# A pre-LayerNorm attention layer: the side products on TensorE cut into 64x32 pieces that stand between the two scores of a unit

## The chip, the cores and the metric

The kernel runs on one core of a Trainium2 chip. The metric is device time in microseconds (us) of the whole program, the median of the runs shown. A profile is of one execution, and its times are of that execution alone.

## What is computed

One layer over x of shape (4, 2048, 256): LayerNorm, attention with 16 heads of 16 channels, the projection added to x, a second LayerNorm, three 256x256 products in a row, tanh, added again.

```python
qkv = einsum('bse,fe->bsf', layernorm(x), in_proj_weight) + in_proj_bias
scores = einsum('bhqd,bhkd->bhqk', q / sqrt(16), k)
blocked = (j <= i) & (j >= i - 16)          # keys just before the query are left out
attn = softmax(where(blocked, -inf, scores))
x = x + einsum('bse,fe->bsf', attn @ v, out_proj_weight) + out_proj_bias
h = layernorm(x) @ ffn_weight @ ffn_aux_weight1 @ ffn_aux_weight2
return x + tanh(h + ffn_bias)
```

## The kernel before

`first_batch` prepares batch 0: LayerNorm, query, key and value projections. Then `stream` runs 16 **steps**, one for each chunk of 512 queries (4 batches x 4 chunks). A step has 64 **units** (`STEP`), numbered r = 0 to 63 here; a unit is 64 keys against 512 queries for 8 heads, 32 units for each half of the heads. On PE a unit is: first scores (`score(u, 0)`, 8 products of a 49x32 weight tile with 512 fp16 columns into two banks), the weighting of an earlier unit (`weigh`, 8 products of 64x32 with 512 fp32 columns, three or four units behind), and second scores (`score(u, 1)`, two other banks). ScalarE takes each pair of banks with one exponential of 128x1024, two a unit, 2048 in all. `score` waits for the exponential that last read its banks. VectorE multiplies out the blocked band (`mask`) in the units 15 to 23 of each half, two units behind the exponential and before the weighting. Position 13 of each half has two weightings, position 3 none.

Beside that, TensorE has **side work**, hung behind the second scores of units that `run_step` lists by number. In the first 12 steps (`PROJECTED`) it projects the chunk of the next batch: `turn` (transposes of the normalised chunk), `project_qk` for four blocks j, `project_v`, and `sum_squares` for the norms that set the softmax guard. In all steps but the first it finishes the chunk before: `project_out`, `f_turn`, `project_f`. These are 128x128 or 128x64 products over a contraction of 256, in two halves k. All of them use two spare PSUM banks, `spare[0]` and `spare[1]`, one product in each, which VectorE takes with one operation (`take_qk`, `take_v`, `take_norms`, `add_attention`, `add_f_bias`); the next user of a bank waits for that.

The order on each engine is written by hand, and a wait blocks all that stands behind it on its engine. SyncE issues all DMAs in one queue: queries for the next half, the context rows out of `raw` (`move_context`), the softmax sums and their inverses (`invert_sums`), the chunk of x for the finish (`start_chunk`), the projected parts (`store_part`), the result (`store_result`), and at a batch's end the keys of the next batch (`load_keys`, 1.5 MB for each half of the heads in pieces of few bytes: half 0 late in the last step, half 1 at the next step's start).

The lines of `run_step` on PE that set the place of side work:

```python
                    score(u, 0)
                    due = weighed_at(u)
                    if due:
                        weigh(due[0])
                    score(u, 1)
                    for w in due[1:]:
                        weigh(w)
                    if projects and r in (8, 9):
                        turn(step, r - 8)
                    if projects and r in (12, 14):
                        project_qk(step, 0, (r - 12) // 2)
```

Lines of the profile: L1135 scores, L1154 weighting, L1113 exponential, L1105 tanh, L1183 and L1248 turns, L1195 queries and keys, L1211 values, L1224 norms, L1237 output projection, L1257 last product, L837 mask, L897, L902 and L906 queries and keys on VectorE.

## Time and profile before

| | us |
|---|---|
| median of 3 runs | 2204.01 (2202.97 to 2208.4) |
| the profiled execution | 2206.76 |
| its span, first to last instruction | 2202.9 |
| ScalarE busy | 1987.1 (90%) |
| PE busy | 1903.6 (86%) |
| VectorE busy | 587.1 (27%) |

Busy time of PE counts pipelined matmuls with their whole latency, so 86% is not 86% of its peak. A float32 product shows as two matmul records and two weight loads. The loop over units runs from 87.8 to 2144.2 us; ahead of it is `first_batch`, behind it the finish of the last chunk.

### The profile page before, as it was taken

To read this page: it belongs to the slowest core of one execution; us is meant where nothing else is said; L and a number is where in the kernel's file an instruction comes from. 1 tells how busy PE (TensorE), PEld (TensorE's weight loads), DVE (VectorE), ACT (ScalarE), POOL (GpSimd) and SP (SyncE) were. 2 spreads that over 40 slices of the span, in tenths; PEclk is the share of its full clock that TensorE was granted. 3 is DMA by queue.
4 is the path that set the end of the run, shared out by engine and by line. 5 is a ranking of instruction groups with operands and counts; after the bars stand their busy time and mean duration, and the time that the engine had idled before them with its cause. 6 is when DMAs were issued, how large, how long until landed. Compare 5 with 4: busy or idle time off the path is not lost. (4 is left out here: it accounts for less than half of the span.)

```text
span 2202.9 us, 76197 instructions
## 1 busy us (share of the span) xinstructions
PE 1903.6 (86%) x34896; PEld 677.2 (31%) x34896; DVE 587.1 (27%) x1206; ACT 1987.1 (90%) x2106; POOL 149.9 (7%) x172
## 2 busy tenths in 40 slices
PE   6698998989889898999889899898988888888882
PEld 4232332323323233333323333232332222222221
DVE  5221323223222332323223232222311111111212
ACT  3499999999889999999889999999989999999990
POOL 2000101001000000101001010100100000000000
PEclk9799999999999999999999999999999999999995
DMA  3410102011240111102331010201123010101000
GB/s 120 128 31 15 44 24 63 25 54 31 44 81 24 54 33 34 44 12 63 53 67 48 24 43 24 64 24 44 32 41 64 15 44 14 44 15 34 16 23 27
DMA packets 84927, 92.81 MB, mean 42 GB/s; under 512 B 15786, under 2 KB 73578, under 8 KB 84594
## 3 DMA queue, kind: packets, MB, share of 16 engines
q1 hardware_dynamic: 84596, 87.83, 16.0%
q8 instruction: 277, 4.54, 0.9%
q14 instruction: 54, 0.44, 0.1%
HBM read 53.09 MB, written 26.25 MB: 36 GB/s over the span
## 5 line engine op out<-in xcount | busy, mean ns | idle before, releaser
L1113 ACT ACTIVATE probs<-scores 128x1024 f32<-128x1024 f32 x2048 | 1948.6, 1056 | 117.8 <-PE scores L1135 80.7
L1154 PE MATMUL outs<-probs,vs 64*32 64x512 f32 x16384 | 1081.0, 593 | 7.7 <-issue 7.7
L1135 PE MATMUL scores<-qs,ks 49*32 49x512 f16 x16384 | 839.9, 384 | 231.2 <-ACT probs L1113 180.7
L1135 PEld LDWEIGHTS scores<-qs,ks 49*32 49x32 f16 x16384 | 233.4, 89 | 1250.6 <-ACT probs L1113 1093.5
L1154 PEld LDWEIGHTS outs<-probs,vs 64*32 64x32 f32 x16384 | 291.2, 106 | 74.3 <-issue 30.7
L837 DVE TENSOR_TENSOR probs<-probs,allowed 128x320 f32<-128x320 f32 (+2 forms) x280 | 138.6, 495 | 388.1 <-ACT probs L1113 388.1
L1195 PE MATMUL spare<-s_xt,w_qkv 128*128 128x512 f32 x192 | 108.0, 645 | 0.0
L786 POOL TENSOR_TENSOR s_squares<-s_qk_f 128x512 bf16<-128x512 f32 x48 | 61.4, 1279 | 464.1 <-DVE s_qk_f L897 464.1
L1237 PE MATMUL spare<-w_o,ctx_in 128*128 128x256 f32 x256 | 74.1, 416 | 19.0 <-DVE ctx_in L862 19.0
L897 DVE TENSOR_SCALAR s_qk_f<-spare,bias_qk 128x512 f32<-128x512 f32 x48 | 36.0, 751 | 182.1 <-PE spare L1195 182.1
L1257 PE MATMUL spare<-w_ffn,s_f_xt 128*128 128x256 f32 x256 | 74.0, 415 | 0.8 <-DVE s_f_xt L977 0.8
L780 POOL TENSOR_TENSOR s_x<-s_x,bias_o 128x1024 f32<-128x1024 f32 x16 | 38.1, 2379 | 486.3 <-DMA s_x<-in_x 486.3
L845 DVE COPY raw<-outs 128x512 f32<-128x512 f32 x32 | 22.1, 692 | 172.5 <-PE outs L1154 171.6
L977 DVE COPY s_f_xt<-spare 128x512 f32<-128x512 f32 x32 | 22.1, 692 | 138.4 <-PE spare L1248 138.4
L1237 PEld LDWEIGHTS spare<-w_o,ctx_in 128*128 128x128 f32 x256 | 45.4, 196 | 38.5 <-DVE ctx_in L862 19.9
L1105 ACT ACTIVATE s_pre<-s_pre 128x1024 f32<-128x1024 f32 x16 | 17.7, 1107 | 41.2 <-DVE s_pre L983 41.2
L1211 PE MATMUL spare<-w_qkv,s_xt 128*64 128x128 f32 x768 | 53.4, 282 | 0.0
L988 DVE TENSOR_TENSOR s_pre<-s_pre,s_x 128x1024 f32<-128x1024 f32 x16 | 19.6, 1226 | 124.8 <-ACT s_pre L1105 124.8
L1257 PEld LDWEIGHTS spare<-w_ffn,s_f_xt 128*128 128x128 f32 x256 | 45.3, 196 | 19.7 <-issue 14.3
L906 DVE SCALAR_TENSOR_TENSOR s_parts<-s_qk_f,s_parts 128x512 f16<-128x512 f32 x48 | 50.2, 1045 | 0.8
L947 DVE TENSOR_TENSOR s_x<-s_x,spare 128x512 f32<-128x512 f32 x32 | 22.0, 688 | 99.7 <-PE spare L1237 99.7
L1211 PEld LDWEIGHTS spare<-w_qkv,s_xt 128*64 128x64 f32 x768 | 41.7, 138 | 15.7 <-issue 15.7
(97 smaller groups left out, 566.5 us busy)
## 6 DMA issues: line engine op xcount, KB each, us to landing
qs<-q_parts SPq DMA_DIRECT2D x192, 64.0 KB
ks<-k_parts SPq DMA_DIRECT2D x36, 256.0 KB
ctx_in<-raw SPq DMA_DIRECT2D x256, 32.0 KB, 2.0
s_x<-in_x SPq DMA_DIRECT2D x16, 512.0 KB, 4.0
inverse<-row_inverse SPq DMA_DIRECT2D x32, 256.0 KB
out<-s_pre SPq DMA_DIRECT2D x16, 512.0 KB, 2.9
s_xin<-in_x SPq DMA_DIRECT2D x12, 512.0 KB, 6.0
q_parts<-s_parts SPq DMA_DIRECT2D x24, 256.0 KB, 2.1
```

What stands on the lines that cost most here:

```text
L780: pool.tensor_tensor(x2[:], x2[:], bias, ALU.add).then_inc(biased, 1)
L786: pool.tensor_tensor(squares[:, j], qk_f[:, j % 2], qk_f[:, j % 2], ALU.mult).then_inc(squared, 1)
L837: dve.tensor_tensor(tiles, tiles, keep_row, ALU.mult).then_inc(masked, 1)
L897: dve.tensor_scalar(qk_f[:, j % 2], spare[j % 2][:], HD ** -0.5 if j < HALVES else 1.0, bias_qk[:, j:j + 1], ALU.mult, ALU.add).then_inc(q ...
L906: dve.scalar_tensor_tensor(out=parts[:, j, 1], in0=qk_f[:, j % 2], scalar=SCALE_UP, in1=parts[:, j, 0], op0=ALU.mult, op1=ALU.subtract).th ...
L1113: act.activation(probs[:, u % RING, 2 * slot:2 * slot + 2].rearrange("p c q -> p (c q)"), scores[:, 2 * slot:2 * slot + 2].rearrange("p c ...
L1135: last = pe.matmul(scores[cols, 2 * slot + e], ks[rows, group, keys], qs[rows, group], start=True, stop=True)
L1154: last = pe.matmul(outs[32 * c:32 * c + 32, side], vs[keys, at:at + 2 * HD], probs[keys, u % RING, c], start=(i == 0), stop=(i == KBLOCKS ...
L1195: last = pe.matmul(spare[j % 2][:], w_qkv[:, k, j * P:(j + 1) * P], xt[:, k], start=(k == 0), stop=(k == HALVES - 1))
L1211: last = pe.matmul(spare[1 - two // 2][side * HALF_P:(side + 1) * HALF_P, kb % 4 * P:(kb % 4 + 1) * P], xt[:, k, kb * KEYS:(kb + 1) * KEYS ...
L1237: last = pe.matmul(spare[t // 2][:, t % 2 * EMB:(t % 2 + 1) * EMB], ctx_in[:, k, t * P:(t + 1) * P], keep["w_o"][:, k], start=(k == 0), st ...
L1257: last = pe.matmul(spare[1 - t // 2][:, t % 2 * EMB:(t % 2 + 1) * EMB], f_xt[:, k, t * P:(t + 1) * P], keep["w_ffn"][:, k], start=(k == 0) ...
```

## The change

Every side product is made of pieces of the shape of the weighting: `product` and `turned_tiles` cut a 128x128 product into four column groups (32 outputs) and two row groups (64 of the contraction), 8 products that write `spare[0]` (rows 0 to 63 of the contraction) and `spare[1]` (rows 64 to 127). The two banks together now hold one product as two partial sums, and VectorE takes it with two operations, where the transposes are copied bank by bank. A piece of queries, keys, output projection or last product has 256 columns and one half k; there are four for each pair of banks. A turn's piece has 16 products of 64 columns, a piece of values 16 of 128, `sum_squares` 8 bf16 products of 512. Tables say at which unit each piece stands (25 units before, 60 now in a step that projects and finishes), and the last product of a chunk reaches into the step after the next one's start (places over 63).

In a unit with a piece PE's order is first scores, piece, second scores, weighting; in one without it stays as it was. VectorE, ScalarE (the tanh stands at unit 8 of the next step, or at 58) and SyncE follow the tables. On SyncE `store_result(step - 2)` and `start_chunk` stand behind `invert_sums`, and `move_context(step, 0)` ahead of the key parts. The folding of the three weights (`fold_ffn`, twice in step 0) keeps its 128x128 form.

```diff
+TURN_AT = (7, 8, 9, 10)
+QK_AT = ((12, 14, 15, 16), (18, 19, 20, 21), (33, 34, 35, 36), (38, 39, 40, 41))
+FOLD_AT = (23, 28)
+Y_AT = ((23, 24, 25, 26), (28, 29, 30, 31))
+V_AT = ((43, 44, 46, 47), (51, 52, 53, 54))
+NORM_AT = 49
+F_TURN_AT = {True: (56, 57, 58, 59), False: (41, 42, 43, 44)}
+F_AT = {True: ((61, 62, 63, 64), (66, 67, 68, 69)), False: ((47, 48, 49, 50), (52, 53, 54, 55))}
+SQUASH_AT = {True: 72, False: 58}
...
@@ SyncE, run_step @@
-                    start_chunk(step - 1)
                     move_context(step - 1, 1)
                     invert_sums(step - 1)
+                    if step > 1:
+                        store_result(step - 2)
+                    start_chunk(step - 1)
...
@@ VectorE, take_qk @@
-                dve.tensor_scalar(qk_f[:, j % 2], spare[j % 2][:], HD ** -0.5 if j < HALVES else 1.0,
-                                  bias_qk[:, j:j + 1], ALU.mult, ALU.add).then_inc(qk_copied, 1)
+                dve.tensor_scalar(qk_f[:, j % 2], spare[0][:], scale, bias_qk[:, j:j + 1], ALU.mult, ALU.add
+                                  ).then_inc(qk_added, 1)
+                dve.wait_ge(qk_added, n + 1)
+                dve.scalar_tensor_tensor(out=qk_f[:, j % 2], in0=spare[1][:], scalar=scale, in1=qk_f[:, j % 2],
+                                         op0=ALU.mult, op1=ALU.add).then_inc(qk_copied, 1)
...
@@ VectorE, take_norms @@
+                dve.tensor_copy(both, spare[0][0:HALF_P]).then_inc(norms_added, 1)
+                dve.wait_ge(norms_added, 2 * step + 1)
+                dve.tensor_tensor(both, both, spare[1][0:HALF_P], ALU.add).then_inc(norms_added, 1)
...
@@ PE @@
+            def turned_tiles(tiles, pair, k):
+                for t in (2 * pair, 2 * pair + 1):
+                    for c in range(4):
+                        for part in range(2):
+                            rows = slice(part * HALF_P, part * HALF_P + HALF_P)
+                            at = (k * TPC + t) * HALF_P
+                            last = pe.matmul(spare[part][32 * c:32 * c + 32, at:at + HALF_P],
+                                             tiles[rows, t, k * P + 32 * c:k * P + 32 * c + 32], ident[rows, rows],
+                                             start=True, stop=True)
+                return last
+
+            def product(at, weights, moving, k):
+                for c in range(4):
+                    for part in range(2):
+                        rows = slice(part * HALF_P, part * HALF_P + HALF_P)
+                        last = pe.matmul(spare[part][32 * c:32 * c + 32, at:at + EMB], weights(rows, c), moving[rows],
+                                         start=(k == 0), stop=(k == HALVES - 1))
+                return last
...
@@ PE, project_qk @@
+                n, k = divmod(i, HALVES)
...
+                    else:
+                        pe.wait_ge(qk_copied, step * 4 + j)
+                last = product(n * EMB, lambda rows, c: w_qkv[rows, k, j * P + 32 * c:j * P + 32 * c + 32],
+                               xt[:, k, n * EMB:(n + 1) * EMB], k)
...
@@ PE, run_step @@
-                    score(u, 0)
                     due = weighed_at(u)
-                    if due:
-                        weigh(due[0])
-                    score(u, 1)
-                    for w in due[1:]:
-                        weigh(w)
...
+                    score(u, 0)
+                    if has_piece(step, r):
+                        piece(step, r)
+                        score(u, 1)
+                        for w in due:
+                            weigh(w)
+                    else:
+                        if due:
+                            weigh(due[0])
+                        score(u, 1)
+                        for w in due[1:]:
+                            weigh(w)
```

The order on PE in step 1, from the second scores of unit 12 to the first half of block 0's second piece in unit 14, before. The names are written<-read; a count stands for equal neighbours:

```order
L1135 MATMUL scores<-qs,ks 32x512 x8
L1195 MATMUL spare<-s_xt,w_qkv 128x512
L1135 MATMUL scores<-qs,ks 32x512 x8
L1154 MATMUL outs<-probs,vs 32x512 x8
L1135 MATMUL scores<-qs,ks 32x512 x8
L1154 MATMUL outs<-probs,vs 32x512 x8
L1135 MATMUL scores<-qs,ks 32x512 x8
L1154 MATMUL outs<-probs,vs 32x512 x8
L1135 MATMUL scores<-qs,ks 32x512 x8
L1195 MATMUL spare<-s_xt,w_qkv 128x512
```

The same place now, from unit 11's second scores on:

```order
L1172 MATMUL scores<-qs,ks 32x512 x16
L1230 MATMUL spare<-s_xt,w_qkv 32x256 x8
L1172 MATMUL scores<-qs,ks 32x512 x8
L1191 MATMUL outs<-probs,vs 32x512 x8
L1172 MATMUL scores<-qs,ks 32x512 x8
L1191 MATMUL outs<-probs,vs 32x512 x8
L1172 MATMUL scores<-qs,ks 32x512 x8
L1191 MATMUL outs<-probs,vs 32x512 x8
L1172 MATMUL scores<-qs,ks 32x512 x8
L1230 MATMUL spare<-s_xt,w_qkv 32x256 x8
L1172 MATMUL scores<-qs,ks 32x512 x8
```

The piece moved from behind a unit's second scores to between its scores, and the weighting of such a unit moved behind the second scores.

VectorE in a later step, from the turned chunk to the first block of queries, before:

```order
L889 COPY s_xt<-spare 128x512 x2
L862 TENSOR_TENSOR ctx_in<-ctx_in,inverse 128x512 x2
L897 TENSOR_SCALAR s_qk_f<-spare,bias_qk 128x512
L902 TENSOR_SCALAR s_parts<-s_qk_f 128x512
L906 SCALAR_TENSOR_TENSOR s_parts<-s_qk_f,s_parts 128x512
L837 TENSOR_TENSOR probs<-probs,allowed 128x4x16
L837 TENSOR_TENSOR probs<-probs,allowed 128x4x80 x2
```

and now:

```order
L913 COPY s_xt<-spare 128x8x64 x2
L860 TENSOR_TENSOR probs<-probs,allowed 128x4x16
L924 TENSOR_SCALAR s_qk_f<-spare,bias_qk 128x512
L927 SCALAR_TENSOR_TENSOR s_qk_f<-spare,s_qk_f 128x512
L932 TENSOR_SCALAR s_parts<-s_qk_f 128x512
L860 TENSOR_TENSOR probs<-probs,allowed 128x4x80
L936 SCALAR_TENSOR_TENSOR s_parts<-s_qk_f,s_parts 128x512
```

Block 0 is taken with one operation more (L927, from `spare[1]`), and the scaling of the context (L862, now L885) has moved behind it.

## Rows read from the trace of the kernel before

**Rows 1.** Page, section 1; groups by line: count | busy us, mean ns | idle
```profile
PE 1903.6 (86%) x34896; PEld 677.2 (31%) x34896; DVE 587.1 (27%) x1206; ACT 1987.1 (90%) x2106; POOL 149.9 (7%) x172
...
L1113 ACT ACTIVATE probs<-scores 128x1024 f32<-128x1024 f32 x2048 | 1948.6, 1056 | 117.8 <-PE scores L1135 80.7
...
L1154 PEld LDWEIGHTS outs<-probs,vs 64*32 64x32 f32 x16384 | 291.2, 106 | 74.3 <-issue 30.7 <-ACT probs L1113 1.1
...
L906 DVE SCALAR_TENSOR_TENSOR s_parts<-s_qk_f,s_parts 128x512 f16<-128x512 f32 x48 | 50.2, 1045 | 0.8
...
L897 DVE TENSOR_SCALAR s_qk_f<-spare,bias_qk 128x512 f32<-128x512 f32 x48 | 36.0, 751 | 182.1 <-PE spare L1195 182.1
```

**Rows 2.** Timeline, ScalarE: start us, us, instruction, count [idle before <- what ended it]
```profile
87.80 2.85 ACT L1113 ACTIVATE probs<-scores 128x1024 f32<-128x1024 f32 x3 [21.50 <-PE scores L1135]
...
860.70 1.11 ACT L1105 ACTIVATE s_pre<-s_pre 128x1024 f32<-128x1024 f32 x1
...
861.64 23.08 ACT L1113 ACTIVATE probs<-scores 128x1024 f32<-128x1024 f32 x25
...
988.36 1.11 ACT L1105 ACTIVATE s_pre<-s_pre 128x1024 f32<-128x1024 f32 x1
...
1893.03 1.11 ACT L1105 ACTIVATE s_pre<-s_pre 128x1024 f32<-128x1024 f32 x1
...
2015.33 1.11 ACT L1105 ACTIVATE s_pre<-s_pre 128x1024 f32<-128x1024 f32 x1
...
2142.19 2.05 ACT L1113 ACTIVATE probs<-scores 128x1024 f32<-128x1024 f32 x2
```

**Rows 3.** Timeline of step 6, units 14 to 18, all engines.
```profile
895.78 0.41 PE L1135 MATMUL scores<-qs,ks 49*32 49x512 f16 x8
...
896.26 3.02 ACT L1113 ACTIVATE probs<-scores 128x1024 f32<-128x1024 f32 x3 [0.38 <-PE scores L1135]
...
897.13 1.41 DVE L906 SCALAR_TENSOR_TENSOR s_parts<-s_qk_f,s_parts 128x512 f16<-128x512 f32 x1
...
898.43 0.40 PE L1135 MATMUL scores<-qs,ks 49*32 49x512 f16 x8
...
898.75 1.12 PE L1195 MATMUL spare<-s_xt,w_qkv 128*128 128x512 f32 x2
...
899.81 0.41 PE L1135 MATMUL scores<-qs,ks 49*32 49x512 f16 x8
...
900.23 0.49 DVE L837 TENSOR_TENSOR probs<-probs,allowed 128x320 f32<-128x320 f32 x1 [1.55 <-ACT probs L1113]
...
900.90 0.88 PE L1135 MATMUL scores<-qs,ks 49*32 49x512 f16 x16
```

**Rows 4.** Timeline of a plain unit of step 7, PE.
```profile
1001.44 0.41 PE L1135 MATMUL scores<-qs,ks 49*32 49x512 f16 x8 [0.51 <-ACT probs L1113]
1001.54 0.27 PEld L1154 LDWEIGHTS outs<-probs,vs 64*32 64x32 f32 x16
```

**Rows 5.** Page, sections 3 and 6; windows (busy us, clock, DMA share, GB/s); timeline
```profile
q8 instruction: 277, 4.54, 0.9%
...
ctx_in<-raw SPq DMA_DIRECT2D x256, 32.0 KB, 2.0
...
549.50:563.50 14.00, 9.73 (x187) 3.24 (x186) 3.89 (x8) 11.01 (x12) 1.17 (x5) 1.00 1.05 136
...
606.50:622.50 16.00, 9.57 (x204) 2.67 (x192) 2.58 (x6) 12.62 (x14) 0.00 (x0) 1.00 0.99 131
...
618.43 0.39 PE L1135 MATMUL scores<-qs,ks 49*32 49x512 f16 x4
624.26 1.04 PE L1135 MATMUL scores<-qs,ks 49*32 49x512 f16 x12 [5.45 <-issue]
```

**Rows 6.** Window and timeline of PE in the tail.
```profile
2160.00:2170.00 10.00, 5.37 (x13) 4.35 (x14) 2.73 (x5) 0.00 (x0) 0.00 (x0) 0.51 0.13 49
...
2164.63 6.25 PE L1237 MATMUL spare<-w_o,ctx_in 128*128 128x256 f32 x16 [19.02 <-DVE ctx_in L862]
```

More of the change, by code:

```diff
@@ L742, in run_step @@
                     load_queries(sp, lay, step + 1, 0, q_parts)
+                move_context(step, 0)
                 if projects:
@@ L1115, in _ @@
                                    ACT.Exp, scale=1.0 / (SCALE_UP * SCALE_UP)).then_inc(exped, 1)
-                if step and r == 60:
-                    squash(step - 1)
+                for c, at, beside in finishing(step, r):
+                    if at == SQUASH_AT[beside]:
+                        squash(c)
             squash(NCH - 1)
@@ L1180, in turn @@
                     if step > 1:
                         pe.wait_ge(pre_done, step * 2 - 2)
[L1182 to L1188 removed]
+                last = turned_tiles(xin, i // 2, i % 2)
+                if i == 3:
+                    last.then_inc(turned, 1)
@@ new lines, in project_qk, with project_v @@
+                last = product(n * EMB, lambda rows, c: w_qkv[rows, k, j * P + 32 * c:j * P + 32 * c + 32],
+                               xt[:, k, n * EMB:(n + 1) * EMB], k)
+                if i == 3:
+                    last.then_inc(qk_ready, 1)
+            def project_v(step, half, i):
+                if i == 0:
+                    if half == 0:
+                        pe.wait_ge(qk_copied, step * 4 + 4)
+                    else:
+                        pe.wait_ge(norms_copied, step * 2 + 2)
+                kb = half * 4 + i
+                for k in range(HALVES):
+                    for c in range(4):
+                        side, part_keys = divmod(c, 2)
+                        keys = slice(kb * KEYS + part_keys * 32, kb * KEYS + part_keys * 32 + 32)
+                        for part in range(2):
+                            rows = slice(part * HALF_P, part * HALF_P + HALF_P)
+                            last = pe.matmul(spare[part][32 * c:32 * c + 32, i * P:(i + 1) * P], xt[rows, k, keys],
+                                             w_qkv[rows, k, 2 * EMB + side * P:2 * EMB + (side + 1) * P],
@@ L1261, in run_step @@
-            def run_step(step):
+                pe.wait_ge(v_copied, step * 2 + 1)
+                for k in range(HALVES):
+                    for w in range(2):
+                        for part in range(2):
+                            rows = slice(part * HALF_P, part * HALF_P + HALF_P)
+                            last = pe.matmul(spare[part][32 * w:32 * w + 32], head_of[rows, k], squares[rows, 2 * w + k],
+                                             start=(k == 0), stop=(k == HALVES - 1))
@@ L1262, in run_step, with piece @@
+            def piece(step, r):
                 projects = step < PROJECTED
@@ L1264, in run_step @@
                 finishes = f >= 0
+                if projects:
+                    if r in TURN_AT:
+                        turn(step, TURN_AT.index(r))
+                    for j in range(4):
+                        if r in QK_AT[j]:
+                            project_qk(step, j, QK_AT[j].index(r))
+                    for half in range(2):
+                        if r in V_AT[half]:
+                            project_v(step, half, V_AT[half].index(r))
+                    if r == NORM_AT:
+                        sum_squares(step)
@@ new lines, in piece @@
+                if step == 0 and r in FOLD_AT:
+                    fold_ffn(FOLD_AT.index(r))
+                for pair in range(2):
+                    if finishes and r in Y_AT[pair]:
+                        project_out(f, pair, Y_AT[pair].index(r))
+                for c, at, beside in finishing(step, r):
+                    if at in F_TURN_AT[beside]:
+                        f_turn(c, F_TURN_AT[beside].index(at))
+                    for pair in range(2):
+                        if at in F_AT[beside][pair]:
+                            project_f(c, pair, F_AT[beside][pair].index(at))
@@ new lines, in has_piece @@
+            def has_piece(step, r):
+                places = []
+                if step < PROJECTED:
+                    places += [TURN_AT, *QK_AT, *V_AT, (NORM_AT,)]
+                if step:
+                    places += Y_AT
+                else:
+                    places.append(FOLD_AT)
+                found = any(r in place for place in places)
+                for _, at, beside in finishing(step, r):
+                    found = found or any(at in place for place in (F_TURN_AT[beside], *F_AT[beside]))
+                return found
```

356 lines of the change are left out of this document (165 added, 191 removed).

## The prediction

> **What bounds the kernel now.** I read the page first, then the groups of instructions by line, then the timeline of one unit, then everything that ScalarE waits for. ScalarE runs 2048 exponentials and is fed for nearly the whole loop [rows 1]. Undisturbed, 25 of them take 23.08 us: (23.08 - 1.06) / 24 = 0.915 us from start to start, 1.83 us a unit of two [rows 2]. A step of 64 units with its tanh (the next exponential starts 0.94 us after it) would then take 64 x 1.83 + 0.94 = 118.1 us. From tanh to tanh, a step that projects takes 988.36 - 860.70 = 127.7 us, and one that doesn't 2015.33 - 1893.03 = 122.3 us [rows 2]. So 9.6 and 4.2 us a step are lost, and PE causes them: per unit it streams 0.22 + 0.22 us of scores and 0.86 us of weighting, 1.3 of 1.83 us, and the side work comes on top.
>
> How a piece costs time is seen in unit 16 of step 6 [rows 3]. Second scores start at 898.43, the 128x128 piece at 898.75 (0.1 us after the scores have streamed), the next first scores only at 899.81. The 512 fp32 columns stream in 0.85 us, so piece and changeovers hold PE for 1.38 - 0.22 = 1.16 us, 0.3 of it at the changes of array shape. The first scores come late. Then the second scores stand behind a weighting: 900.90 - 899.81 = 1.09 us. An exponential starts 0.48 us after its scores (895.78 to 896.26) and runs 1.02 us at least, so ScalarE starves: 0.38 us before 896.26, behind the piece of unit 14 [rows 1, 3].
>
> The chain in numbers, counted from the end of a unit's first exponential as 0. Ends follow each other by 0.915 us. New scores for a bank can start about 0.05 after its exponential has ended, and have to start 0.48 + 1.02 = 1.50 before the end that their own exponential is to have. So the next unit's first scores may start from 0.05 to 2 x 0.915 - 1.50 = 0.33, its second ones from 0.97 to 1.25. In the old order a plain unit has them at 0.05 and 0.05 + 1.09 = 1.14: in time by 0.11, and PE sits idle 0.51 us ahead of the unit [rows 4].
>
> **The change, part by part.**
> *New pieces.* One is 8 products of 64x32 with 256 columns (16 with 64 or 128 columns in the turns and values). The weighting has just this shape with 512 columns: 16 PE records, and it occupies PE for 1.09 - 0.22 = 0.87 us [rows 3]. So 256 columns are 0.43 us; the 128-column pieces (twice the products) 0.43 us; the 64-column ones between 0.21 us by columns and 0.43 us by their four weight loads in turn at 106 ns each [rows 1]. I take 0.43 for all. Below nothing is excluded: the same columns have to pass.
> *New order.* In a unit with a piece the first scores start at 0.05 (0.22 after such a unit), the piece ends 0.65 later, at 0.87 at the latest, and the second scores may only start at 0.97, when their bank is free. The piece fits in a hole, up to 0.53 us long free of charge. The weighting behind it delays the next first scores to 0.97 + 1.09 = 2.06, where 0.915 x 2 + 0.33 = 2.16 is allowed. Price: zero. At the end of a run of pieces two weightings meet around one score: 0.22 + 1.09 = 1.31 against 1.25, 0.06 us, 15 times a step, 0.9 us. The two double weightings a step (position 13 of a half) cost some 0.15 each. A projecting step becomes 118.1 + 1.2 = 119.3 us, another (5 runs) 118.7 us. Gain: 12 x 8.4 + 4 x 3.6 = **115 us**. The weight folding of step 0 keeps its 128x128 form, inside a unit now. Both folds are 4 x 0.43 + 0.3 = 2.0 us on PE before and after, 0.7 beyond any hole in either place; what differs is at most 1 us for both, counted +0.6.
> *VectorE.* Every product is now taken with two operations. For queries and keys 0.75 + 1.05 us (751 and 1045 ns [rows 1]) and about 0.2 of hand-over, after at most 0.5 of mask [rows 3]: 2.5 us, and the next user of the banks stands 3.2 us behind. So it hides. Only the norms chain is tight: two passes and two maxima at about 0.69 are 3.0 us, behind a mask 3.5, against 3.2: 0 to 0.3 us in 12 places, counted as 1 us. VectorE grows from 587 us by some 120 us, far from full.
> *DMA queue.* On SyncE the load of x for the finish now stands behind the context and sums and behind the stored result, so it leaves the first burst of a batch. The key parts are stored after unit 43, so the keys of the next batch load about units 46 to 54 instead of 39 to 46.
> *PE's instructions.* 34896 matmul records and as many loads came in 277 blocks: 252 a block, 1.15 us of transfer each (0.9% x 16 x 2203 / 277) [rows 1, 5]. A unit has 64 records, so a block lasts 7.3 us. At 618.5 us PE stops after 4 of 8 score matmuls, with nothing to wait for but "issue", until 624.26 [rows 5]. DMA was full from 606.5 to 622.5 us. I read this as a block that was asked for when the one before it was begun and queued behind the keys. Such places are the end and the start of a step at the three batch changes. The loop takes 2144.2 - 87.8 = 2056.4 us; less 12 x 127.7 + 4 x 122.3 = 2021.6, that leaves **35 us** for these six [rows 2]. With a burst of length B served at its end plus 1.6 us, and the asking anywhere in the first block's time T, the mean stall is B + 1.6 - 1.5 T: 14 + 1.6 - 11 = 4.6 and 16 + 1.6 - 11 = 6.6 us now, 34 in all, as is there. The new kernel has 96 records in a unit with a piece and 128 in turns and values: T is 4.3 us for the late keys (values stand there) and 4.7 us at a batch's start, whose burst is 2 us shorter. 14 + 1.6 - 6.4 = 9.2 and 14 + 1.6 - 7 = 8.6, three times each: 53 us, 19 more, and 3 for what PE has to make up behind longer stops: **+22**. Bounds: 0 (a trip that can start between the keys' transfers) and +45 (a second dry place in each burst).
> *Blocks elsewhere.* A usual trip isn't in the trace as one duration. It is over 1.15 us and under 7.3, since no stall stands outside the bursts; a small DMA takes 2.0 us from issue to landing [rows 5], so I take 1.15 + 2 = 3.2 us. In the 16 units with 128 records a block lasts 3.7 us, else 4.8. Trips of 3.2 fit; those behind a 256 or 512 KB transfer may not. 24 blocks a step, a few of them 1 us late, half absorbed: **+15 us**, between 0 and 60.
> *Tail.* [...] Two extra waits of a half-speed pair (3.4 us) less what was hidden, plus four additions of 0.69: +3 for the projection, +3 for the last product, +1 for the turns: **+7 us**.
>
> [...] The weighting's 16 loads, those of its second passes among them, are over in 0.27 us, while a first pass of 512 columns needs 0.43 [rows 4]. [...]
>
> **Sum.** -115 + 0.6 + 1 + 22 + 15 + 7 = -69. Against the profiled execution, 2206.8 us (span 2202.9 and 3.9 around it), that is 2137; its median lies 2.8 us lower at 2204.0. I forecast **2134 us**, 3.2% less.
>
> **The rivals.**
> *Blocks stay hidden* (chance 0.13). Neither bursts nor other places grow: -115 + 9 = -106, **2098 us**. For: 271 of 277 blocks cost nothing today. Against: the six dry places. [...]
> *VectorE late between first and second scores* (0.13). A piece's own wait now stands ahead of the second scores, so lateness of VectorE goes straight to ScalarE. The addition L906 shows up to 1.4 us beside GpSimd [rows 3]. 13 hand-overs a step, 12 steps, 0.1 to 0.3 us each: +15 to +45, **2150 to 2180 us**.
> *Weight loads show* (0.05). Pieces of 0.64 to 0.86 us instead of 0.43: 0.11 to 0.33 beyond the free 0.53, less 0.1 of slack, in about 42 units x 12: +10 to +115, **about 2200 us** in the middle.
> *PE's blocks bound it, slower* (0.09). Where the mean trip L of a block exceeds 3.7 us, 96 blocks pay L - 3.7, and beyond 4.8 another 120 pay L - 4.8. It decides from L = 4.6 us: 96 x 0.9 = 86 eats the 84 us left. At 5.0 it is 125 + 24 = 149: **2268 us**. For: trips of 13 us in bursts. Against: no dry place elsewhere, though 7.3 us cannot tell 3 from 5.
> *The change doesn't do what it says* (0.02): pieces wait for one another in order, over 2250 us.
>
> **How the numbers follow.** The forecast has 0.58. Range 2096 to 2185 us: from the hidden blocks to the late VectorE, leaving out some 0.18. A measurement of this kernel can tell 0.3% (6.6 us) from nothing. Faster: forecast, hidden blocks, late VectorE and half of the loads' case, **0.86**; same **0.03**; slower **0.11**.
>
> **What would show it.** Steps of 119 to 120 us between tanhs away from batch changes; exponentials in unbroken groups over units with pieces; second scores 0.92 us after the first in them; side pieces of 0.43 us from scores to scores; some 370 blocks of PE instructions; "issue" stalls of 8 to 9 us at the six batch changes; last exponential near 2070 us. It is wrong if "issue" stands ahead of scores all through a step (blocks), or VectorE ahead of spare's pieces, or if loads of the pieces lie 0.1 us apart.

## The result, and the profile after

The changed kernel takes 2116.82 us (median of 4 runs, 2113.79 to 2123.87), the kernel before, run beside it, 2203.49 (4 runs, 2199.27 to 2208.4). The ratio is 0.961, between 0.9579 and 0.9642: 3.9% faster. The profiled execution took 2113.79 us, of which the span is 2109.7, so against the profiled execution of before (2206.76) the difference is -93.0 us, where the sum of the prediction had -69. The direction was right and the time lies in the range, 17 us below the forecast.

The first view is the page of the changed kernel, section 1 (busy us, share of the span, instructions), the queue of PE's instruction blocks, and the groups by line (busy us, mean ns, idle ahead of them). It answers rows 1 and the first line of rows 5.

```profile
PE 1856.2 (88%) x47072; PEld 761.6 (36%) x47072; DVE 698.6 (33%) x1366; ACT 1936.3 (92%) x2106; POOL 150.7 (7%) x172
...
q8 instruction: 372, 6.09, 1.3%
...
L1149 ACT ACTIVATE probs<-scores 128x1024 f32<-128x1024 f32 x2048 | 1897.3, 1067 | 69.5 <-PE scores L1172 66.1
...
L1230 PE MATMUL spare<-s_xt,w_qkv 64*32 64x256 f32 x3072 | 120.9, 376 | 0.6 <-DVE s_qk_f L927 0.6
```

PE and VectorE have more instructions, as the change says, and ScalarE's idle time ahead of exponentials fell from 117.8 [rows 1] to 69.5 us. The last line is the rival of a late VectorE: PE waited 0.6 us in all for it.

ScalarE's timeline of a step that projects (step 6) answers rows 2: start, length, instruction, count and, in brackets, idle time ahead with what ended it.

```profile
838.80 1.09 ACT L1141 ACTIVATE s_pre<-s_pre 128x1024 f32<-128x1024 f32 x1
839.75 95.06 ACT L1149 ACTIVATE probs<-scores 128x1024 f32<-128x1024 f32 x102
935.02 24.19 ACT L1149 ACTIVATE probs<-scores 128x1024 f32<-128x1024 f32 x26 [0.22 <-PE scores L1172]
959.06 1.09 ACT L1141 ACTIVATE s_pre<-s_pre 128x1024 f32<-128x1024 f32 x1
```

From tanh to tanh this step takes 120.3 us, 127.7 before [rows 2], and its 128 exponentials run on with one gap of 0.22 us. The lengths of all steps, from the first exponential of each to the first of the next (taken from the trace's records of exponentials), in us:

| | steps 0 to 3 | 4 to 7 | 8 to 11 | 12 to 15 | usual projecting / other |
|---|---|---|---|---|---|
| before | 127.3 127.7 127.7 134.8 | 134.3 127.7 127.7 133.7 | 132.7 127.7 127.7 136.5 | 124.2 122.3 122.3 122.5 | 127.7 / 122.3 |
| after | 122.6 118.3 119.5 128.1 | 126.0 119.8 120.3 129.2 | 125.7 119.4 119.8 128.9 | 122.4 119.0 119.0 119.2 | 119.3 / 119.0 |

The last column is not a median of the lengths beside it. It is built of units: for each of the 64 units the median of its length over the steps of its sort, and these added up, so that a stop in a few steps does not count. This sum is called the usual step below. The six whole steps of the changed kernel that project and lie away from batch changes (1, 2, 5, 6, 9 and 10) are 118.3 to 120.3 us, 119.5 on the mean.

PE's timeline over two units with pieces (step 6) answers rows 3 and 4.

```profile
870.74 0.40 PE L1172 MATMUL scores<-qs,ks 49*32 49x512 f16 x8
870.96 0.62 PE L1230 MATMUL spare<-w_o,ctx_in 64*32 64x256 f32 x16
871.48 0.41 PE L1172 MATMUL scores<-qs,ks 49*32 49x512 f16 x8
871.71 1.04 PE L1191 MATMUL outs<-probs,vs 64*32 64x512 f32 x16
872.57 0.40 PE L1172 MATMUL scores<-qs,ks 49*32 49x512 f16 x8
...
874.23 0.41 PE L1172 MATMUL scores<-qs,ks 49*32 49x512 f16 x8 [0.17 <-ACT probs L1149]
...
875.20 0.41 PE L1172 MATMUL scores<-qs,ks 49*32 49x512 f16 x8
```

The piece starts 0.22 us behind the scores (870.96 - 870.74), as the weighting does behind its own (871.71 - 871.48 = 0.23). First scores follow each other by 872.57 - 870.74 = 1.83 us, ScalarE's own pace. The second scores start 0.74 us behind the first inside a run of pieces and 0.97 at its start (875.20 - 874.23); the prediction had 0.92 for all, though its own chain lets a weighting push the first scores back and so gives both. How little a piece needs is seen where no exponential holds the next scores back: a piece of values with 32 records (all engines but VectorE, step 5), 789.25 - 788.82 = 0.43 us.

```profile
788.60 0.58 PEld L1274 LDWEIGHTS spare<-w_qkv,s_xt 64*32 64x32 f32 x32 [0.30 <-issue]
788.82 0.64 PE L1274 MATMUL spare<-w_qkv,s_xt 64*32 64x128 f32 x32
...
789.25 0.42 PE L1172 MATMUL scores<-qs,ks 49*32 49x512 f16 x8
```

What is left of idle time stands at the batch changes. Windows of 2 us across the end of step 3 (busy us of PE, weight loads, VectorE, ScalarE and GpSimd with counts, PE's granted clock, DMA share, GB/s) answer rows 5; then PE's stops of all six changes, and ScalarE's idle time at the first two.

```profile
532.00:534.00 2.00, 2.00 (x56) 0.74 (x48) 0.00 (x0) 2.00 (x3) 0.00 (x0) 1.00 0.99 168
...
540.00:542.00 2.00, 1.39 (x26) 0.31 (x22) 1.72 (x3) 2.00 (x3) 0.00 (x0) 1.00 1.06 131
542.00:544.00 2.00, 0.00 (x0) 0.00 (x0) 1.90 (x6) 0.04 (x1) 0.23 (x1) 1.00 1.01 126
544.00:546.00 2.00, 0.00 (x0) 0.00 (x0) 0.09 (x1) 0.00 (x0) 1.13 (x5) 0.89 0.99 156
546.00:548.00 2.00, 0.86 (x16) 0.52 (x24) 0.00 (x0) 0.00 (x0) 0.00 (x0) 0.50 0.10 19
```

```profile
547.14 1.06 PE L1191 MATMUL outs<-probs,vs 64*32 64x512 f32 x1 [5.61 <-issue]
...
592.56 1.96 PE L1191 MATMUL outs<-probs,vs 64*32 64x512 f32 x16 [5.21 <-issue]
...
1033.83 1.10 PE L1191 MATMUL outs<-probs,vs 64*32 64x512 f32 x7 [1.97 <-issue]
...
1044.92 0.89 PE L1274 MATMUL spare<-w_qkv,s_xt 64*32 64x128 f32 x23 [2.37 <-issue]
...
1089.51 0.53 PE L1219 MATMUL spare<-ident,s_xin 64*32 64x64 f32 x18 [5.13 <-issue]
...
1534.17 0.63 PE L1172 MATMUL scores<-qs,ks 49*32 49x512 f16 x8 [6.40 <-issue]
...
1575.94 0.41 PE L1230 MATMUL spare<-w_ffn,s_f_xt 64*32 64x256 f32 x3 [0.97 <-issue]
...
1584.63 0.40 PE L1172 MATMUL scores<-qs,ks 49*32 49x512 f16 x6 [1.43 <-issue]
```

```profile
549.52 1.02 ACT L1149 ACTIVATE probs<-scores 128x1024 f32<-128x1024 f32 x1 [7.48 <-PE scores L1172]
551.65 36.91 ACT L1149 ACTIVATE probs<-scores 128x1024 f32<-128x1024 f32 x40 [1.11 <-PE scores L1172]
594.99 4.89 ACT L1149 ACTIVATE probs<-scores 128x1024 f32<-128x1024 f32 x5 [6.43 <-PE scores L1172]
```

DMA is full from 532 to 546; PE waits for nothing but "issue" from about 541 until 547, when the keys are through, and then runs at a granted clock of 0.50 until about 552, so that ScalarE loses 7.48 + 1.11 = 8.6 us to a stop of 5.6. Over the six changes PE's stops add up to 29.1 us and ScalarE's gaps to some 41 us.

What happens at these stops stands in the trace's record of DMA packets. Queue 8 is listed as "instruction", and its packets are of 16 KB each. Their number goes with PE's: 277 packets for 2 x 34896 matmul and load records before, 372 for 2 x 47072 here, 428 for 2 x 54240 in e4 and 323 for 2 x 40800 in e10 (pages, sections 1 and 3), 252 to 254 records a packet, while ScalarE has 2106 instructions in all four. So I read them as PE's instructions, one packet a block. Before the first stop one of its packets began at 531.83 and the next only at 543.80. Between them, in the window 533.1 to 543.7, all 427 packets are of the data queue:

```profile
q1 hardware_dynamic: 427, 1.33, 102.1%
```

The packet of 543.80 was over at 545.52, and PE went on at 547.14. So it is at each of the eight stops: PE goes on 1.2 to 1.8 us after a packet of queue 8 is over, and this packet had begun 7 to 13 us after the one before it. With no packet of the data queue between them, those of 927.53 and 930.88 are 3.4 us apart, and PE has no stop. A few us of full DMA need not delay them: with the data queue at 96% between them, those of 967.67 and 971.04 are 3.4 us apart too, and PE has no stop.

The tail answers rows 6 (PE behind the last weighting). The projection, 6.25 us in one go before, is two halves with a wait of 1.64 us for VectorE between them, and the last product has such a wait too.

```profile
2065.90 3.67 PE L1230 MATMUL spare<-w_o,ctx_in 64*32 64x256 f32 x64 [19.34 <-DVE ctx_in L885]
2071.21 3.65 PE L1230 MATMUL spare<-w_o,ctx_in 64*32 64x256 f32 x64 [1.64 <-DVE s_x L989]
...
2089.25 1.96 PE L1230 MATMUL spare<-w_ffn,s_f_xt 64*32 64x256 f32 x64 [1.57 <-DVE s_pre L1032]
```

The books of the two profiled executions: the stretch from the first exponential to the end of the last is 1957.2 us (87.98 to 2045.19), 2056.4 before, so -99.2; what lies behind it grew from 58.7 to 64.5 us, +5.8; what lies ahead and around comes to the rest, +0.4. Sum -93.0.

### The profile page after: what moved, and what is told of

Its sections match the earlier page's. It is cut to its first block and busy times, and to the rows that moved or that the text cites. A ratio compares the mean times of both kernels' runs of the same rounds, so it can differ in the third digit from the quotient of the medians.

```text
span 2109.7 us, 100654 instructions
## 1 busy us (share of the span) xinstructions
PE 1856.2 (88%) x47072; PEld 761.6 (36%) x47072; DVE 698.6 (33%) x1366; ACT 1936.3 (92%) x2106; POOL 150.7 (7%) x172
## 5 line engine op out<-in xcount | busy, mean ns | idle before, releaser
L1149 ACT ACTIVATE probs<-scores 128x1024 f32<-128x1024 f32 x2048 | 1897.3, 1067 | 69.5 <-PE scores L1172 66.1
L1191 PEld LDWEIGHTS outs<-probs,vs 64*32 64x32 f32 x16384 | 307.7, 106 | 74.0 <-issue 29.9
L1230 PE MATMUL spare<-s_xt,w_qkv 64*32 64x256 f32 x3072 | 120.9, 376 | 0.6 <-DVE s_qk_f L927 0.6
L1230 PE MATMUL spare<-w_o,ctx_in 64*32 64x256 f32 x2048 | 81.9, 391 | 21.0 <-DVE ctx_in L885 19.3
L1230 PE MATMUL spare<-w_ffn,s_f_xt 64*32 64x256 f32 x2048 | 81.3, 384 | 3.9 <-DVE s_pre L1032 1.6
L1274 PE MATMUL spare<-w_qkv,s_xt 64*32 64x128 f32 x3072 | 66.0, 274 | 3.7 <-issue 2.8
L1230 PEld LDWEIGHTS spare<-s_xt,w_qkv 64*32 64x32 f32 x3072 | 56.0, 106 | 24.8 <-issue 4.4
L1274 PEld LDWEIGHTS spare<-w_qkv,s_xt 64*32 64x32 f32 x3072 | 51.9, 107 | 21.1 <-issue 7.9
L1029 DVE TENSOR_TENSOR s_pre<-spare,bias_f 128x512 f32<-128x512 f32 x32 | 22.1, 689 | 105.0 <-PE spare L1230 105.0
L1230 PEld LDWEIGHTS spare<-w_o,ctx_in 64*32 64x32 f32 x2048 | 37.4, 110 | 37.6 <-DVE ctx_in L885 20.2
```

The lines of the kernel that those rows point to most:

```text
L1029: dve.tensor_tensor(tiles, spare[0][:].rearrange("p (t e) -> p t e", t=2), keep["bias_f"][:].unsqueeze(1).to_broadcast([P, 2, EMB]), ALU.a ...
L1149: act.activation(probs[:, u % RING, 2 * slot:2 * slot + 2].rearrange("p c q -> p (c q)"), scores[:, 2 * slot:2 * slot + 2].rearrange("p c ...
L1191: last = pe.matmul(outs[32 * c:32 * c + 32, side], vs[keys, at:at + 2 * HD], probs[keys, u % RING, c], start=(i == 0), stop=(i == KBLOCKS ...
L1230: last = pe.matmul(spare[part][32 * c:32 * c + 32, at:at + EMB], weights(rows, c), moving[rows], start=(k == 0), stop=(k == HALVES - 1))
L1274: last = pe.matmul(spare[part][32 * c:32 * c + 32, i * P:(i + 1) * P], xt[rows, k, keys], w_qkv[rows, k, 2 * EMB + side * P:2 * EMB + (sid ...
```

## The experiments

All eight ran beside the kernel before, in two groups (its median was 2204.81 us in the first, 2206.39 in the second). Ratios are to it, with their 95% interval. "After" is the changed kernel, 2116.82 us.

**The order undone (e1_old_order).** After, with the piece behind the second scores again.

```diff
                     score(u, 0)
+                    if due:
+                        weigh(due[0])
+                    score(u, 1)
+                    for w in due[1:]:
+                        weigh(w)
                     if has_piece(step, r):
                         piece(step, r)
-                        score(u, 1)
...
```

> The changed kernel with the 64x32 pieces at the same units, but PE's order in them as before: first scores, weighting, second scores, piece. Theory A (the size and shape of the piece make the gain): second scores at 1.14 us, streamed at 1.36, a piece of 0.43 ends at 1.79, and the next first scores may only start at 1.83 + 0.05. The piece fits behind the second scores as well as ahead of them: steps of 118 to 119.5 us instead of 119.3, 2105 to 2118 us. Theory B (the new order makes the gain): each of 44 pieces a step delays the next first scores by 0.2 us or more as the old pieces did, 2170 to 2215 us.

Measured 2108.28 us (2100.6 to 2116.5), ratio 0.9565 (0.9523 to 0.9607). ScalarE in step 6 has no gap at all:

```profile
835.88 1.15 ACT L1141 ACTIVATE s_pre<-s_pre 128x1024 f32<-128x1024 f32 x1
836.82 118.03 ACT L1149 ACTIVATE probs<-scores 128x1024 f32<-128x1024 f32 x128
954.64 1.15 ACT L1141 ACTIVATE s_pre<-s_pre 128x1024 f32<-128x1024 f32 x1
```

This step is 118.8 us; the usual step of both sorts is 118.7. So the whole gain is there without the new order, and by the traces 0.6 us a projecting step more: the loss at the end of each run of pieces (below) is gone. The intervals of the two kernels overlap, so the 8 us between the medians show nothing by themselves; what the order costs is told by the step lengths, and by e9 below, which has the old order and is faster than e6, which has the new one.

**The order alone (e2_big_between).** The kernel before, with its 128x128 pieces at their old units, but between the two scores.

```diff
+                    score(u, 0)
+                    if has_piece(step, r):
+                        piece(step, r)
+                        score(u, 1)
+                        for w in due:
+                            weigh(w)
...
```

> The kernel before with its own 128x128 and 128x64 pieces at their own units, but in such a unit the new order: first scores, piece, second scores, weighting. Theory A: a piece of 1.16 us in a hole of 0.53 makes the second scores 0.18 us late, the next first scores 0.36 and the second scores behind them 0.54, against 0.37 a piece before: not faster, 2205 to 2255 us. Theory B: the order alone brings most of the gain, 2120 to 2170 us.

Measured 2202.88 us (10 runs, 2199.29 to 2210.35), ratio 0.9991 (0.9975 to 1.0008), steps 127.6 and 122.3. The order is worth nothing to the big pieces either. That is 2 us under the range of 2205 to 2255: my 0.54 us a piece was too high. My reading, which no run tests by itself, is that a piece longer than the hole costs the same in both places, 1.16 us of PE time against what the two units around it leave free. Together the two runs give the whole change to the pieces' form.

**Form or length (e10_big_shape).** After, where `product` is one 128x128 product of 256 columns into `spare[0]`. The share of `spare[1]` is left out; VectorE still adds that bank, so its work is the same.

```diff
-                for c in range(4):
-                    for part in range(2):
...
+                return pe.matmul(spare[0][:, at:at + EMB], weights, moving, start=(k == 0), stop=(k == HALVES - 1))
```

> The changed kernel, but the pieces of queries, keys, output projection and last product are 128x128 products of the same 256 columns into one bank; the second bank's share is left out (VectorE still adds what is in it). The streaming time is the same 0.43 us, the instructions fewer; what is back is the change of array shape, 0.3 us a piece. If the shape matters: 0.74 us in a hole of 0.53, 0.1 to 0.3 us late in each of 32 units a step, 2150 to 2200 us. If only the size of the piece matters: 2110 to 2118 us.

Measured 2169.19 us (2165.1 to 2170.8), ratio 0.9828 (0.9811 to 0.9845): 52 us slower than after, with as many columns in each piece. PE and its weight loads in step 6:

```profile
890.69 0.40 PE L1172 MATMUL scores<-qs,ks 49*32 49x512 f16 x8
...
891.02 0.30 PEld L1227 LDWEIGHTS spare<-w_o,ctx_in 128*128 128x128 f32 x2 [0.39 <-issue]
891.02 0.70 PE L1227 MATMUL spare<-w_o,ctx_in 128*128 128x256 f32 x2
...
891.65 0.41 PE L1172 MATMUL scores<-qs,ks 49*32 49x512 f16 x8
...
892.74 0.40 PE L1172 MATMUL scores<-qs,ks 49*32 49x512 f16 x8
```

The piece starts 0.33 us behind the scores instead of 0.22, and the scores 0.63 behind it instead of 0.43: the 128x128 form costs 0.11 + 0.20 = 0.3 us, the figure that the prediction read from rows 3 and put on the change of array shape. The run doesn't tell that change from the weight load: the loads of the 128x128 piece begin with it at 891.02, while those of a 64x32 piece begin with the scores ahead of it (0.22 us sooner at 870.74). The unit takes 892.74 - 890.69 = 2.05 us instead of 1.83. Usual steps are 123.7 and 121.6 us.

**The size of the hole (e5_long_qk).** After, with pieces of queries and keys of 512 columns instead of 256, as many instructions (the product is made twice).

```diff
-                last = product(n * EMB, lambda rows, c: w_qkv[rows, k, j * P + 32 * c:j * P + 32 * c + 32],
-                               xt[:, k, n * EMB:(n + 1) * EMB], k)
+                for c in range(4):
+                    for part in range(2):
+                        rows = slice(part * HALF_P, part * HALF_P + HALF_P)
+                        last = pe.matmul(spare[part][32 * c:32 * c + 32], w_qkv[rows, k, j * P + 32 * c:j * P + 32 * c + 32],
+                                         xt[rows, k], start=(k == 0), stop=(k == HALVES - 1))
```

> The changed kernel, but each piece of queries and keys has 512 columns instead of 256 (the same product is made twice over its four places, with the same number of instructions): 0.86 instead of 0.43 us. By the hole that the prediction reckons with (0.53 us free) PE then has 0.22 + 0.86 + 0.22 + 0.86 = 2.16 us in a unit of 1.83: +0.33 us in each of 16 units of 12 steps, less a first one that slack takes, +50 to +63 us, 2165 to 2185 us. If the piece is hidden whatever its length: 2117 us.

Measured 2161.11 us (2160.04 and 2162.18), ratio 0.9798 (0.9778 to 0.9817).

```profile
884.49 0.41 PE L1172 MATMUL scores<-qs,ks 49*32 49x512 f16 x8
884.71 1.05 PE L1259 MATMUL spare<-s_xt,w_qkv 64*32 64x512 f32 x16
885.57 0.41 PE L1172 MATMUL scores<-qs,ks 49*32 49x512 f16 x8
...
886.65 0.41 PE L1172 MATMUL scores<-qs,ks 49*32 49x512 f16 x8
```

Such a unit takes 886.65 - 884.49 = 2.16 us: PE has no free moment, 0.22 + 0.86 + 0.22 + 0.86. That is 0.33 over ScalarE's pace, for 0.43 more columns. So the hole is 1.83 - 1.3 = 0.53 us, as forecast, and the 256-column piece leaves 0.1 of it. The first piece of a run was nearly free, which is why 44 us were lost and not the 48 to 68 of the expectation, whose range of 2165 to 2185 us is missed by 4.

**More records, the same columns (e4_more_records).** After, with products of 128 columns instead of 256 and twice as many of them: 128 PE records in such units, 428 blocks instead of 372.

```diff
+            def small(at, weights, moving):
+                for k in range(HALVES):
+                    for c in range(4):
+                        for part in range(2):
...
+                            last = pe.matmul(spare[part][32 * c:32 * c + 32, at:at + P], weights(rows, k, c),
+                                             moving(rows, k), start=(k == 0), stop=(k == HALVES - 1))
```

> The changed kernel, but every piece of queries, keys, output projection and last product has both halves of the contraction and 128 columns instead of one half and 256: the same columns, twice the instructions (128 PE records in nearly each unit with a piece). Theory A with blocks of instructions of some 3.2 us of trip against 3.7 us that a block then lasts: the batch changes lose 45 to 55 instead of 42 us and a few blocks elsewhere are late, 2122 to 2150 us. If blocks are no limit: 2117 us. If a trip is 4 us or more on the mean: over 2160 us.

Measured 2134.56 us (2133.56 to 2139.04), ratio 0.9681 (0.9653 to 0.9709), 18 us slower than after, with the same usual steps (119.3 and 119.1). The stops at the batch changes grew, from 29.1 to 37.2 us in all (the second was 5.21), and short gaps of ScalarE, 0.8 to 1.9 us, now stand alone in steps 3, 5, 7, 9, 10 and 11. The second stop; then, for the lone gap of step 10, ScalarE, PE and the data queue in the window 1353.1 to 1359.6:

```profile
599.47 1.96 PE L1191 MATMUL outs<-probs,vs 64*32 64x512 f32 x16 [7.75 <-issue]
```

```profile
1362.97 1.02 ACT L1149 ACTIVATE probs<-scores 128x1024 f32<-128x1024 f32 x1 [1.66 <-PE scores L1172]
...
1362.26 0.33 PE L1239 MATMUL spare<-s_xt,w_qkv 64*32 64x128 f32 x7 [1.73 <-issue]
...
q1 hardware_dynamic: 1456, 1.71, 88.9%
```

So the blocks do cost more where PE goes through more of them (428 and 37.2 us, against 372 and 29.1), and the lone gaps go with late packets too. In all six PE goes on 1.2 to 1.5 us after a packet of queue 8 is over, and that packet began 7.2 to 8.3 us after the one before, behind 0.7 to 1.5 MB of data in the 5 us ahead of it (in step 10 the finished chunk going out and two chunks of x coming in, 512 KB each). The rate alone isn't what fails: elsewhere in this run such packets follow each other by 3.3 to 3.9 us more than a hundred times, and PE doesn't stop.

**The keys spread (e6_keys_apart, e8_before_keys_apart).** The keys of the next batch are loaded in four parts of 512 tokens, 4 to 10 units apart, instead of at once; e6 does so in the changed kernel, e8 in the kernel before. The bytes are the same.

```diff
+            def key_part(b, hg, k):
+                load_keys(sp, lay, b, hg, k_parts, slice(k * CHUNK, (k + 1) * CHUNK))
...
-                        load_keys(sp, lay, b, 1, k_parts, slice(0, SEQ))
...
+                        key_part(b, 1, 2)
...
+                        sp.wait_ge(scored, 2 * (STEP * step + 11))
+                        key_part(b, 1, 3)
...
+                        sp.wait_ge(scored, 2 * (STEP * step + 16))
+                        key_part(b, 1, 0)
```

> The changed kernel with the keys of the next batch loaded in four parts of 512 tokens (the same bytes), 4 to 10 units apart, instead of in one burst for each half of the heads. Theory A (a block of PE's instructions waits behind the burst): bursts of 3.5 us instead of 14 to 16, so most of the 42 us that the six places lose comes back, 2080 to 2095 us. Rival (the stop at a batch change has another cause, such as the guard, the keys' own lateness or the sums): 2110 to 2125 us, with the stops where they were.

> The kernel before, with the keys of the next batch loaded in four parts that stand apart. If its six stops of 35 us are the same wait for a block of instructions behind the burst: 2168 to 2178 us. If they are something else: 2200 us or more.

Measured 2070.21 us (2068.88 to 2070.47), ratio 0.9389 (0.9362 to 0.9415), for e6, and 2173.66 (2172.74 to 2174.0), ratio 0.9855 (0.9838 to 0.9871), for e8. Three lines of e6, from the page and from windows across the places of the first two stops; then e8's windows at the times of rows 5:

```profile
L1174 ACT ACTIVATE probs<-scores 128x1024 f32<-128x1024 f32 x2048 | 1894.5, 1069 | 28.7 <-PE scores L1197 26.3
...
530.00:550.00 20.00, 19.42 (x598) 9.00 (x584) 8.05 (x18) 19.94 (x23) 1.76 (x5) 1.00 0.20 53
575.00:593.00 18.00, 16.57 (x480) 6.96 (x472) 4.45 (x9) 18.00 (x20) 0.00 (x0) 1.00 0.32 87
```

```profile
549.50:563.50 14.00, 12.96 (x266) 4.62 (x260) 3.89 (x8) 13.84 (x16) 1.17 (x5) 1.00 0.16 46
606.50:622.50 16.00, 14.04 (x282) 4.55 (x266) 1.93 (x5) 15.95 (x18) 2.37 (x1) 1.00 0.35 99
```

No "issue" stop of PE over 0.4 us is left in the loop of e6, and none in that of e8. All of e8's steps are 127.7 or 122.3 us (step 0 127.3, step 15 122.5), all of e6's between 118.3 and 120.7 (step 0 121.9). The 33 us that e8 gains are the 35 that the prediction had put down to six stops from one row and a subtraction; in the changed kernel the same cause was worth 47. That is more than was expected of e6 (2080 to 2095 us, from 42 us lost): the granted clock is now 1.00 from 98.3 us to the end of the loop, where the changed kernel had 0.50 for 3.4 or 6.8 us behind each of its six stops of 2 us and more, so with PE's stops the slow way back behind them is gone too.

**All together (e9_big_tail).** The old order, the keys spread, and for the last chunk the 128x128 products of before with one bank for each pair.

```diff
-            for n in range(TPC * HALVES):
-                project_out(f, n // 4, n % 4)
...
+            for pair in range(2):
+                for half in range(2):
+                    t = 2 * pair + half
+                    for k in range(HALVES):
+                        last = pe.matmul(spare[pair][:, half * EMB:(half + 1) * EMB], ctx_in[:, k, t * P:(t + 1) * P],
+                                         keep["w_o"][:, k], start=(k == 0), stop=(k == HALVES - 1))
+                last.then_inc(y_ready, 1)
```

> The changed kernel with three edits: PE's old order in units with a piece (first scores, weighting, second scores, piece), keys in four parts, and for the last chunk, behind the loop, the 128x128 products of the kernel before with one bank each. By the sums so far 2070 (keys apart), less 0.5 us a step for the order (118.7 instead of 119.3 us a step), less the 5.8 us that the tail has grown: 2056 us, 2050 to 2064. If order and keys do not add up or the pairs of the tail overlap anyway: 2064 to 2072 us.

Measured 2058.54 us (2055.94 to 2064.48), ratio 0.9339 (0.9317 to 0.936). It is the fastest version, 58 us below after and 12 below e6. Its loop, from the first exponential to the end of the last, is 1906.3 us, 1913.2 in e6: the old order is worth 6.9 us there. Its usual steps are 118.7 us, and the projection of the last chunk is again one go:

```profile
2017.06 6.40 PE L1432 MATMUL spare<-w_o,ctx_in 128*128 128x256 f32 x16 [19.50 <-DVE ctx_in L910]
```

From the last exponential to the last instruction outside SyncE it is 45.8 us, 51.5 in after and 45.1 before.

## Why the prediction was right, and where its sum was not

Each term of the sum, against the step table and the books above:

| term | forecast | measured |
|---|---|---|
| steps, 12 x and 4 x | -115 | 12 x (119.3 - 127.7) + 4 x (119.0 - 122.3) = -114 |
| step 0, folds | +0.6 | +3.7 |
| norms chain | +1 | 0 |
| batch changes | +22 | +8.5 |
| late blocks elsewhere | +15 | +2 |
| tail | +7 | +5.8 |
| sum | -69 | -93.0, the terms to within 1 |

*The steps.* 119.3 us was forecast and is the usual step; the other steps, forecast at 118.7, take 119.0. Three readings carried it, and each has its run: the 1.83 us of a unit and the hole of 0.53 in it (e5), the 0.3 us of the 128x128 form (e10), and 0.43 us for a piece. The chain of allowed starts named the ends of runs as the only place with a price, 0.06 us each. They do lose, but more: eleven lose 0.14 to 0.18 us and two 0.10, and the two double weightings lose 0.26 and 0.28 instead of 0.15, 2.7 us a step where 1.2 was forecast. That the step still came out as forecast is due to the other units, which run at 1.81 us and not 1.83; why they do is not shown. The floor of 118.1 was itself low: (23.08 - 1.06) / 24 is 0.9175 and not 0.915, which gives 118.4, and the steps without any gap in e1 take 118.7. So the mechanism of the steps is right, and that 119.3 came out to the tenth is luck.

*The order.* The prediction explained the gain by piece and order together. e1 and e2 show that the order has no part in it, and costs the ends of runs. In the old order first scores, weighting, second scores and piece (0.22 + 0.87 + 0.22 + 0.43 = 1.74 us) fit into 1.83 us too; there the piece's 0.43 us fill what had been PE's idle time ahead of the unit [rows 4]. The prediction costed only the new place and never the old one with small pieces, so it couldn't see this.

*Step 0.* The term was for the folds alone, and they stayed within the 1 us allowed: the two units with a fold take 3.02 and 3.14 us, 3.11 and 2.90 before, +0.15. What was missed is that step 0 doesn't finish a chunk: it had ten of the 25 big pieces fewer before and so less to gain, 127.3 - 122.6 = 4.7 us instead of 8.4. (The tables of the change give 49 units with a piece to a step that projects and finishes, not 60.)

*Norms chain.* It is seen on the weight loads of the piece behind the norms, which wait for VectorE's maxima (`s_qk_sq`) ten times, 3.9 us in all and 0.4 at most. No gap of ScalarE follows, so the term is nothing.

*Batch changes: the step that was mis-sized.* That the stops come with the bursts is shown by e6 and e8, where none over 0.4 us is left, and by the packets of queue 8, 1.2 to 1.8 us behind whose end PE goes on. When a block is asked for is in no trace; "when the one before it was begun" was my estimate of it, and the formula rests on that. The loss was forecast as 53 us, 8.6 and 9.2 a place, by a formula for the mean stop. The steps at batch changes lie 35.4 us over the usual ones before and 43.9 after (less 0.9 for the tanh that moved from step 1 to step 12). PE's stops were 5.6, 5.2, 2.0 + 2.4, 5.1, 6.4 and 1.0 + 1.4 us, not 8 to 9. What failed is "served at its end": in seven of the eight stops the block's packet began 1.2 to 12 us before the burst was over. So in step 7 a block came through at 1030.11 while DMA was full until 1042, and one long stop became two short ones; in step 12 the same happened.

That the formula gave 34 us for the kernel before, "as is there", was luck. Those 35 us are what ScalarE lost; PE's own stops there were 4.37, 5.45, 4.05, 2.38, 5.65 and 0.98, 22.9 us in all, and the other 12.5 were lost behind them, while PE made up its lag, for some 3 to 7 us of it at a granted clock of 0.50. In the changed kernel the stops are 29.1 us (+6.2, where +19 was forecast) and the rest 14.8 (+2.3, where +3 was forecast). No run shows what sets the place of a block's request within a burst. e1, with the same 372 blocks, has stops of 33.6 us, so the size for one given kernel stays open within some 10 us.

*Late blocks elsewhere: mis-sized.* 15 us were forecast, and the steps 1, 2, 5, 6, 9 and 10 lie 1.3 us over the usual step in sum, 2.2 without that tanh. The trip was taken as 3.2 us against blocks of 3.7 and 4.8, with losses in a few places a step. Behind packets of queue 8 that follow each other by 3.4 to 3.9 us PE has no stop here, so such blocks come in time; those of e4's six lone gaps stand behind large transfers (0.7 to 1.5 MB in 5 us), as the prediction's "those behind a 256 or 512 KB transfer may not" has it. There one lone gap came in each of six steps; here two of PE's stops for "issue" over 0.1 us stand outside the bursts, 0.39 us at 190.48 and 0.15 at 1553.67, both with no data between the packets ahead of them. This term and the one before were 26 us too high together, 2 more than the sum missed by; step 0 went the other way.

*The rivals.* Hidden blocks (2098 us) was half true: elsewhere yes, but for stops of 0.39 and 0.15 us, in bursts no; there they were worth 33 us before and 47 after (e8, e6). A late VectorE is excluded by PE's 0.6 us of waiting for it in the loop. Weight loads that show: 32 loads of a piece, those of its second passes among them, were over in 0.58 us and the piece in 0.43 from scores to scores, with no time for loads of 106 ns in turn. (The 0.64 us put on this rival are 0.43 and two loads of 106 ns [rows 1]; with one it would be 0.43 + 0.11 = 0.54, at the very edge of the hole.) Blocks that bound PE all through didn't come.

*The tail.* +5.8 against +7: two halves with waits of 1.64 and 1.57 us for VectorE. No run shows a clock in GHz behind the half-speed pair of the forecast (3.4 us); what the runs show is a granted clock of 0.51 there before [rows 6] and, after, pairs of 3.67 and 3.65 us at 0.50 and one of 1.96 at 1.00. e9 takes it back.

## What to carry to other kernels

Work that fills in beside a paced engine was free here only below the hole that the pace leaves (0.53 us; a piece of 0.86 cost 0.33 a unit in e5): work out the hole from the timeline of one undisturbed unit, cut the pieces below it, and give them the array shape of their neighbours (0.3 us a piece in e10); where they then stand between these mattered little (0.6 us a step in e1). Look at every stop that waits for "issue" while DMA is full: a bulk load that isn't urgent, cut in four and spread, gave back more here (33 and 47 us) than the stops themselves (22.9 and 29.1 us), since the slow way back behind them went too. The stops grew with the number of instructions that PE gets (22.9, 29.1 and 37.2 us with 277, 372 and 428 blocks), though unevenly (29.1 and 33.6 in two kernels with the same number).

## What the runs showed of the hardware

- PE stood still for "issue" in the bursts of bulk loads: with DMA at 1.0 for 12 to 15 us, for 1.0 to 6.4 us at a time (7.8 in e4), and with the same bytes at a share of 0.16 to 0.35 (e6, e8) for no more than 0.4. At all eight stops of after PE went on 1.2 to 1.8 us after a packet of queue 8 (16 KB, 1.1 us long in the median) was over. In the first burst these packets began 12 us apart, with none but data packets between; without data between them, 3.4 at 927.53.
- Behind transfers of 512 KB the same was seen on a smaller scale: in e4 six packets of queue 8 came 7.2 to 8.3 us after the one before, behind 0.7 to 1.5 MB in 5 us, and PE stood still for 0.9 to 1.7 us.
- The granted clock fell behind the longer stops. In after PE stood still from about 541; its granted clock was 1.00 until 545, 0.50 when it went on at 547, and 1.00 again some 5 us later. So it was, for 3.4 or 6.8 us, at all six stops of 2 us and more, and not at those of 0.97 and 1.43. The kernel before had a clock of 0.64 from 624.3 to 628, behind its stop. Mean clock of the span: 0.974 in after, 0.982 in e6.
- 0.3 us for one 128x128 product amid 64x32 ones (0.11 ahead, 0.20 behind; change of shape and longer load not told apart), 52 us over the kernel (e10).
- The 64x32 products took their time by their columns, also at 128 of them: 32 records of 128 in 0.43 us (after), 16 of 512 in 0.86 (e5). And e4, with the same columns in twice the records, has the same usual steps; what it is slower by goes with the stops for "issue", 37.2 us at the batch changes against 29.1, and the lone gaps.
